# Two expert layers: the low-rank inputs turned between the main tiles, and the last tile in two quarters

## The reference, cut to what matters

```python
x = x + L0_attn(L0_cond(x))
x = x + L0_ffn(L0_cond2(x))      # expert layer 0
x = x + L1_attn(L1_cond(x))
x = x + L1_ffn(L1_cond2(x))      # expert layer 1, the last step

# expert layer 0: 1024 tokens of 512, 8 experts of rank 16, the best 2
gates = relu(layernorm(xf @ gw1.T + gb1) * gamma + beta) @ gw2.T + gb2
top_v, top_i = top_k(gates, 2)
top_g = softmax(top_v)
counts = onehot(top_i).sum(axis=0)        # tokens by expert, over all tokens
w = onehot, weighted by top_g, where counts <= capacity
out = xf @ weight.T + ((xf @ lora_A) * w) @ lora_B * ALPHA

# expert layer 1
combine = the two largest of softmax(x @ W_router.T), divided by their sum
out = x @ W_base.T + b_base + ((x @ A) * combine) @ B * SCALING
```

## Time and profile before

| | |
|---|---|
| median of 3 runs | 1014.01 us (1013.42 to 1014.83) |
| the profiled execution | 1012.35 us, its span 1010.6 us |
| PE busy | 957.1 us (95% of the span) |
| DVE busy | 556.2 us (55%) |
| POOL busy | 469.1 us (46%) |
| ACT busy | 232.3 us (23%) |
| expert layer 0, first main tile to the end of the sixth low-rank product | 652.9 to 686.7 us |
| expert layer 1, first main tile to the first of the final turns | 964.2 to 1003.1 us |

### The profile page before, as it was taken

How to read it: one execution, slowest core, us unless ns; L and a number is a source line. 1 busy time by engine, 2 the same in 40 slices (tenths; PEclk the granted TensorE clock), 3 DMA queues, 4 the chain that set the end, 5 groups by cost and what they waited for, 6 DMA issues and landing times.

```text
span 1010.6 us, 15965 instructions
## 1 busy us (share of the span) xinstructions
PE 957.1 (95%) x6766; PEld 712.3 (70%) x6766; DVE 556.2 (55%) x951; ACT 232.3 (23%) x451; POOL 469.1 (46%) x425
## 2 busy tenths in 40 slices
PE   6899999999999999999999879989989999899997
PEld 2337887877887788887888658846857777446953
DVE  7866748567284753848458435243347969302423
ACT  4602122211122212022120210110052666500001
POOL 7934538485575846758376332301322645220300
PEclk9999999999999999999999989989999999999999
DMA  5782101111110111110113075393470000072002
GB/s 137 177 248 67 57 1 43 73 42 53 43 42 32 42 53 42 73 42 2 53 42 111 17 150 152 84 225 55 185 271 1 3 3 3 2 162 67 4 1 83
DMA packets 36287, 74.30 MB, mean 74 GB/s; under 512 B 13492, under 2 KB 22260, under 8 KB 33140
## 3 DMA queue, kind: packets, MB, share of 16 engines
q1 hardware_dynamic: 35880, 72.89, 25.9%
q10 hardware_dynamic: 336, 0.39, 0.1%
HBM read 66.26 MB, written 7.01 MB: 73 GB/s over the span
## 4 chain that ended last, share of the span: by engine, by line
PE 73%; DVE 11%; POOL 6%; ACT 4%; issue 3%; DMA 1%; SPq 0%; POOLq 0%; DVEq 0%; ACTq 0%
PE ps L1208 15%; PE ps L1146 14%; PE ps L1007 8%; PE ps L1462 5%; PE ps L1280 5%; PE ps L1160 4%; POOL w_lo L2354 3%; DVE arena L2010 3%; ACT acts L1507 2%; PE ps L1385 2%; DVE arena L2007 2%; PE ps L1285 1%; DVE h_lo L2019 1%; PE ps L1387 1%; PE ps L1386 1%
## 5 line engine op out<-in xcount | busy, mean ns | idle before, releaser
L2469 POOL TENSOR_TENSOR arena<-arena 128x512 f32<-128x512 f32 x80 | 103.6, 1295 | 122.7 <-DVE arena L2010 122.6
L1146 PE MATMUL ps<-xt_hi,w_hi 128*128 128x512 f32 x320 | 127.8, 399 | 5.5 <-POOL w_lo L2354 2.7
L1146 PE MATMUL ps<-xt_lo,w_hi 128*128 128x512 f32 x320 | 125.5, 392 | 0.0
L1146 PE MATMUL ps<-xt_hi,w_lo 128*128 128x512 f32 x320 | 125.2, 391 | 0.0
L1208 PE MATMUL ps<-h_hi,wo_hi 128*128 128x512 f32 x256 | 104.9, 410 | 11.9 <-DVE h_lo L2019 11.9
L2028 DVE TENSOR_TENSOR fresh<-ps,fresh 128x512 f32<-128x512 f32 x56 | 38.7, 691 | 133.9 <-PE ps L1208 133.8
L2010 DVE TENSOR_TENSOR arena<-ps,rope 64x512 f32<-64x512 f32 x160 | 110.2, 689 | 2.2
L1208 PE MATMUL ps<-h_lo,wo_hi 128*128 128x512 f32 x256 | 103.1, 403 | 0.0
L1208 PE MATMUL ps<-h_hi,wo_lo 128*128 128x512 f32 x256 | 102.4, 400 | 0.0
L2377 POOL TENSOR_TENSOR xt<-arena 128x512 f32<-128x512 f32 x24 | 30.5, 1270 | 136.9 <-DVE arena L1915 136.9
L1600 ACT ACTIVATE h_hi<-ps 128x512 fp32r<-128x512 f32 x64 | 33.1, 603 | 203.1 <-PE ps L1193 203.1
(11 more groups left out here) (325 smaller groups left out, 1882.8 us busy)
## 6 DMA issues: line engine op xcount, KB each, us to landing
acts<-in_w_o_dram SPq DMA_DIRECT2D x8, 1024.0 KB, 5.0
arena<-in_a_wo_dram SPq DMA_DIRECT2D x8, 1024.0 KB, 5.9
arena<-kernel_rows SPq DMA_DIRECT2D x11, 512.0 KB, 11.7
acts<-in_w_qkv_dram SPq DMA_DIRECT2D x3, 1792.0 KB, 7.0
acts<-in_w_qkv_dram SPq DMA_DIRECT2D x4, 1280.0 KB, 6.6
w_l<-kernel_rows SPq DMA_DIRECT2D x10, 512.0 KB, 11.8
arena<-level_rows SPq DMA_DIRECT2D x4, 1024.0 KB, 21.8
stream<-in_x_dram SPq DMA_DIRECT2D x4, 512.0 KB, 6.7
```

What stands on the lines that cost most here:

```text
L1146: last = pe.matmul(ps[:, bank, :], w[:, r, cols], x, start=(r == 0 and n == 0), stop=(r == R - 1 and n == 2))
L2469: pool.tensor_tensor(qk[:, chunk, half * HALF:(half + 1) * HALF], rot[:, k % 2, 0, :], rot[:, k % 2, 1, :], ALU.add).then_inc(s_rope, 1)
```

## The change

In both expert layers the products keep their number and their operands but for the last tile of layer 1. What changes is where they stand:

- **Layer 0.** `main(0)` to `main(3)`, the count, `main(4)`, the turns of the weighted inputs, `main(5)`, then `lora(0)` to `lora(5)`. The rest is as before.
- **Layer 1.** `main(0)` to `main(2)`, the turns of the weighted inputs, `main(3)`, `lora(0)` to `lora(3)`. Then `main(4)`, turns back of groups 0 and 1, `lora(4)`, `main(5)`, turns back of groups 2 and 3, `lora(5)`. For tile 6 `lora` opens the bank and `main` closes it.
- **Tile 7 of layer 1** is made in two quarters of 256 tokens, low-rank product first: the first in tile 7's bank, the second in tile 4's, behind a wait for tile 4's copy. DVE copies the first (8 samples), ACT the second, with a new instruction. The turn of group 6 waits for that copy.
- On DVE in layer 1 the adds of groups 0 to 3 stand ahead of tile 5's copy, not tile 7's.
- **Output.** Five transfers: three of two groups, then two of one group each.

```diff
--- before.py
+++ after.py
@@ -896,11 +896,12 @@
             load_kernel(3, 2)
             load_levels(3)
             patch(3)
-            for i in range(NGROUP // 2):
-                pair = slice(2 * i * G, 2 * (i + 1) * G)
-                sp.wait_ge(s_added[3], 2 * i + 2)
-                sp.dma_start(out[:, pair, :], stream[:, pair, 1:T + 1]).then_inc(s_out, 16)
-            sp.wait_ge(s_out, 16 * (NGROUP // 2))
+            pieces = (0, 2, 4, 6, 7, 8)
+            for first, end in zip(pieces, pieces[1:]):
+                samples = slice(first * G, end * G)
+                sp.wait_ge(s_added[3], end)
+                sp.dma_start(out[:, samples, :], stream[:, samples, 1:T + 1]).then_inc(s_out, 16)
+            sp.wait_ge(s_out, 16 * (len(pieces) - 1))
 
         N_SETUP = 16 * 3
 
@@ -1274,40 +1275,79 @@
                 for m in range(NTILE):
                     token_products(m)
 
-                def main(k):
+                def main(k, behind=False):
                     half, r_out = k // 4, k % 4
+                    if k in (4, 5):
+
+                        pe.wait_ge(s_natc[n], k - 3)
                     for r in range(R):
-                        pe.matmul(ps[:, FFN_BANK[k], :], w_main[:, r, r_out, :],
-                                  xt[:, r, half * HALF:(half + 1) * HALF], start=(r == 0), stop=False)
-
-                def lora(k):
+                        last = pe.matmul(ps[:, FFN_BANK[k], :], w_main[:, r, r_out, :],
+                                         xt[:, r, half * HALF:(half + 1) * HALF], start=(r == 0 and not behind),
+                                         stop=(r == R - 1 and behind))
+                    if behind:
+                        last.then_inc(s_ffn[n], 1)
+
+                def lora(k, ahead=False):
                     half, r_out = k // 4, k % 4
-                    pe.matmul(ps[:, FFN_BANK[k], :], w_out[:, r_out, :], lora_t[:, half * HALF:(half + 1) * HALF],
-                              start=False, stop=True).then_inc(s_ffn[n], 1)
-
-                for k in range(6):
-                    if k >= 4:
-
-                        pe.wait_ge(s_natc[n], k - 3)
-                    main(k)
-                pe.wait_ge(s_natc[n], 4)
+                    last = pe.matmul(ps[:, FFN_BANK[k], :], w_out[:, r_out, :],
+                                     lora_t[:, half * HALF:(half + 1) * HALF], start=ahead, stop=not ahead)
+                    if not ahead:
+                        last.then_inc(s_ffn[n], 1)
+
+                def last_quarter(q):
+
+                    bank, r_out = (FFN_BANK[7], FFN_BANK[4])[q], R - 1
+                    cols = slice(HALF + q * HALF // 2, HALF + (q + 1) * HALF // 2)
+                    if q:
+                        pe.wait_ge(s_fact[n], 3)
+                    pe.matmul(ps[:, bank, 0:HALF // 2], w_out[:, r_out, :], lora_t[:, cols], start=True, stop=False)
+                    for r in range(R):
+                        last = pe.matmul(ps[:, bank, 0:HALF // 2], w_main[:, r, r_out, :], xt[:, r, cols],
+                                         start=False, stop=(r == R - 1))
+                    last.then_inc(s_ffn[n], 1)
+
+                def turn_weighted():
+                    pe.wait_ge(s_natc[n], 4)
+                    pe.wait_ge(s_lora[n], 1)
+                    for m in range(NTILE):
+                        last = pe.transpose(ps[:, 2 + m // 4, (m % 4) * P:(m % 4 + 1) * P],
+                                            nat[:, m, lora_at:lora_at + P], ident[:, :])
+                        if m % 4 == 3:
+                            last.then_inc(s_lturn[n], 1)
+
                 if n == 0:
+                    for k in range(4):
+                        main(k)
+                    pe.wait_ge(s_natc[n], 4)
                     pe.wait_ge(s_both, 1)
                     pe.matmul(ps[:, 2, 0:P], ones[:, :], both.rearrange("p m k e -> p (m k e)"),
                               start=True, stop=True).then_inc(s_count, 1)
-                pe.wait_ge(s_lora[n], 1)
-                for m in range(NTILE):
-                    last = pe.transpose(ps[:, 2 + m // 4, (m % 4) * P:(m % 4 + 1) * P],
-                                        nat[:, m, lora_at:lora_at + P], ident[:, :])
-                    if m % 4 == 3:
-                        last.then_inc(s_lturn[n], 1)
+                    main(4)
+                    turn_weighted()
+                    main(5)
+                    pe.wait_ge(s_lcopy[n], 2)
+                    for k in range(6):
+                        lora(k)
+                    for k in range(6, 8):
+                        main(k)
+                        turn_first(net, ((s_fact[n], 2), (s_fdve[n], 2)), (2 * k - 12, 2 * k - 11))
+                        lora(k)
+                    return
+                for k in range(3):
+                    main(k)
+                turn_weighted()
+                main(3)
                 pe.wait_ge(s_lcopy[n], 2)
-                for k in range(6):
+                for k in range(4):
                     lora(k)
-                for k in range(6, 8):
+                for k in (4, 5):
                     main(k)
-                    turn_first(net, ((s_fact[n], 2), (s_fdve[n], 2)), (2 * k - 12, 2 * k - 11))
+                    turn_first(net, ((s_fact[n], 2), (s_fdve[n], 2)), (2 * k - 8, 2 * k - 7))
                     lora(k)
+                lora(6, True)
+                main(6, True)
+                for q in range(2):
+                    last_quarter(q)
 
             def attention1():
                 def project(m):
@@ -1484,6 +1524,8 @@
             for what in (s_fact[1], s_fdve[1]):
                 pe.wait_ge(what, 4)
             for g in range(NGROUP // 2, NGROUP):
+                if g == NGROUP - 2:
+                    pe.wait_ge(s_fact[1], 5)
                 turn(3, g)
 
 
@@ -1639,6 +1681,11 @@
                                    ps[:, FFN_BANK[k], :].rearrange("p (b c) -> p b c", c=C),
                                    ACT.Identity, bias=f1_bias[:, 0, r_out:r_out + 1] if n else 0.0)\
                         .then_inc(s_fact[n], 1)
+                if n:
+                    act.wait_ge(s_ffn[n], 9)
+                    act.activation(fresh[:, 24:32, R - 1, :],
+                                   ps[:, FFN_BANK[4], 0:HALF // 2].rearrange("p (b c) -> p b c", c=C),
+                                   ACT.Identity, bias=f1_bias[:, 0, R - 1:R]).then_inc(s_fact[n], 1)
 
             def attention1():
                 def copy_projection(q):
@@ -2189,11 +2236,12 @@
                 (gate0, gate1)[n]()
                 for k in range(1, 8, 2):
                     half, r_out = k // 4, k % 4
-                    for g in range(4 if k == 7 else 0):
+                    for g in range(4 if k == (7, 5)[n] else 0):
                         add_back(2 * n + 1, g)
                     dve.wait_ge(s_ffn[n], k + 1)
-                    dst = fresh[:, half * 16:half * 16 + 16, r_out, :]
-                    src = ps[:, FFN_BANK[k], :].rearrange("p (b c) -> p b c", c=C)
+                    samples = 8 if n and k == 7 else 16
+                    dst = fresh[:, half * 16:half * 16 + samples, r_out, :]
+                    src = ps[:, FFN_BANK[k], 0:samples * C].rearrange("p (b c) -> p b c", c=C)
                     if n:
                         last = dve.tensor_scalar(dst, src, f1_bias[:, 0, r_out:r_out + 1], None, ALU.add)
                     else:
```

## The result

| | before | changed |
|---|---|---|
| median of the runs | 1014.42 us (1013.42 to 1015.97, 4 runs) | 1005.12 us (1001.70 to 1005.42, 4 runs) |
| profiled execution | 1012.35 us, span 1010.6 | 1005.09 us, span 1003.3 |
| layer 0, first main tile to the end of the sixth low-rank product | 33.76 | 27.04 |
| layer 1, first main tile to the first final turn | 38.85 | 36.98 |
| from there to the end of the span | 7.51 | 7.25 |

The ratio is 0.990, with a 95% interval of 0.9884 to 0.9916: the change gains 9.3 us at the median, where 8.8 was forecast. The kernel before has one more run here than the three that the forecast went by; against their 1014.01 the gain is 8.9.

A forecast was written before the change was run, and what follows sets the result against it. The prediction took the tensor engine's chain, 73% of the span, as the bound. Gains of 6.90 (layer 0), 1.90 (layer 1) and 0 (output), 8.80 in all, off the 1014.01 median gave 1005.2 us, range 1003.2 to 1008.3.

The forecast's parts named there:

- Layer 0, 6.90: Expert layer 0, first main tile to last low-rank product: 26.86 us for 33.76, from 3.20 weights standstill, 0.68 copies, 3.03 clock.
- Its third term, 3.03 for the clock: Layer 0's turns (1.98 to 0.87 us) and 12 low-rank passes (7.07 to 5.15) would run at full clock.
- Layer 1, 1.90: Expert layer 1, first main tile to first final turn: 36.95 us for 38.85, a gain of 1.90.
- Behind it, 0: After the first final turn, splitting the output into five transfers gives 0; bounds 0.9 gain, about 0.1 loss.
- What follows moves along: Work behind layer 0, including attention 1's loads, moves 6.9 us earlier; the load queue is free 9.8 us before wanted.
- Rival 5: Attention 1's weights come from a queue still full, layer 0's gain is waited away, 1.9 stays: 1012.1 us, chance 0.02.
- Rival 1: One more fall of the clock elsewhere, as in attention 1, costing about 3.0 us: 1008.2 us, chance 0.15.
- one of the prediction's own signs of being wrong: Signs: layer 0's turns wait beyond some tenths, 256-column passes over 0.22 us, new clock falls, a gap before the last transfer.
- Rival 2: The clock fall at 855 us in attention 1 goes away, worth 1.5 us: 1003.7 us, chance 0.08.
- Rival 3: The half-size last output transfer sets the end, gaining two thirds of 0.9 us: 1004.6 us, chance 0.08.
- Rival 4: Layer 0 gives its standstills but not the clock's 3.0 us: 1008.2 us, chance 0.05.
- Rival 6: Slower: several clock falls at attention 1's heads, 840 to 870 us, at 3.03 each: 1017.3 us, chance 0.02.

The follow-up runs named there:

- e2: Changed kernel with expert layer 0 back in its old order, so only layer 1 and the output change: median 1011.44 us, ratio 0.9975 to the kernel before.
- e3: Kernel before with three unused 512-column products put behind the count of layer 0 to fill the wait: median 1013.08 us, ratio 1.0.
- e10: e3 with four more unused products of 128 columns behind the three, filling the wait longer: median 1013.74 us, ratio 0.9986 to the kernel before.
- e11: The same kernel as e3, run again for another profiled execution: 1009.11 us in that execution, layer 0 31.30 us.
- e1: Kernel before with the new order in expert layer 0 alone: median 1008.13 us, ratio 0.9944 to the kernel before.
- e4: Changed kernel with the output in four transfers of two groups: median 1005.84 us, ratio 0.9915 to the kernel before.
- e9: Changed kernel with two of main tile 4's four products in layer 0 moved behind the turns: median 1006.07 us, ratio 0.9925 to the kernel before.
- e5: Changed kernel with layer 1's tile 7 whole (512 columns), copied by the vector engine alone: median 1005.06 us, ratio 0.9912 to the kernel before.
- e12: The changed kernel again, unaltered, for another profiled execution: span 1002.0 us; the changed kernel's median with it is 1005.09 us.
- e6: Changed kernel with the output in six transfers, groups 4 and 5 sent apart too: median 1003.88 us, ratio 0.9902 to the kernel before.

## Why the prediction was right, point by point

- **Layer 0, 6.90.** Measured 6.72. The order of the pieces came as worked out, and the vector engine's chain ended where it should, with the 0.17 by which the layer began later. What the sum lacked is that the turns' first weight load came only 0.03 ahead of the tile's end, and that cost 0.19. No standstill came of it.
- **Its third term, 3.03 for the clock,** is right in kind in every trace (e2 pays it, e3, e10 and e11 don't), but not all of it is the clock: in e3, at full clock behind the same waits, the turns took 1.09 and the passes 5.42, so the clock's part is 2.5 and 0.5 is the restart behind a wait. The changed kernel won back the restart of the passes (5.15) and not that of the turns (1.06), 2.84 in all. Carried over to medians the term is not confirmed: filling the wait moved the median by 0.4 us at most. The means of all executions, 1013.8 before and 1004.2 changed, are 9.6 apart. By the line above about 6.0 of this is at equal time at half clock, near the standstills of 3.9 and the 2.1 of layer 1 and the end, and 3.6 is for 9.7 us less at half clock (29.8 to 20.1). Of those 9.7, the fall in layer 0 was about 7 in the trace of before (0.93 over 650 to 700, and 1.00 now). But e1, e3 and e10, which are without that fall too in their traces, come down only to 26 us or so. The changed kernel and its variants e4 to e9 have 20.8 over 30 executions, so the low figure is not an accident of five; what brings the rest of it is open. That the forecast for the median came out within 0.1 us is therefore luck in part: the two layers' sums are shown, the account of the clock over the whole execution is not.
- **Layer 1, 1.90.** Measured 1.87. The 256-column passes took 0.216 for 0.215. The last copy's cover held with 0.8 to spare.
- **Behind it, 0.** Measured 0.26. Of this 0.2 is the first add, which starts 0.48 after the first final turn for 0.67, since that turn no longer follows idle time (in e5, where it does, it is 0.67 again). That was missing in the sum. The split of the output was 0, as taken (e4).
- **What follows moves along.** It did: 267.22 before and in e12. Rival 5 is out.
- **Rival 1** happened in the profiled execution, and with it one of the prediction's own signs of being wrong, a fall of the clock where there was none before, for half of its price: 1.4 us for a second fall of about 3.5 us at half clock, not 3.0. The price had been taken from layer 0, where the clock stayed down twice as long. In attention 1, 8 of the 13 kept traces have more than the one fall that the trace of the kernel before has, so a chance of 0.15 for one more was no fit description: such falls move single times by some us, and the median only where their mean number changes. Rival 2 did not happen: no kept trace is without a fall there.
- **Rival 3** falls with e4: four transfers end as late as five. Rival 4's 1008.2 is not what the median came to, but whether all timed executions of the kernel before had the fall in layer 0 is open. Rival 6 was nowhere near.

## What to carry to other kernels

When a helper engine's result is wanted by the tensor engine, don't put all the independent work ahead of the request: ask for the result as soon as its inputs are there, and leave one piece of work for each hand-over. Read a tail of transfers as a block: where it is unbroken, as here, look for what would start it earlier (e6) before cutting the last transfer (e4, nothing). Where single executions of one kernel differ by more than the effect, compare stretches of traces, and note how long the clock was down in each.

## What the runs showed of the hardware

- Every execution spent some of its time at half clock, 14 to 37 us of about 1005. In layer 0 it was full with the engine idle for 1.71 us (e9) and fell with 3.2 (before) and 3.3 (e2).
- The traces of e3, e10 and e11 are without the fall of about 7 us at half clock in layer 0, but their kernels' executions were on average only 3 to 4 us less at half clock. Whether the others have more falls elsewhere or still have that one is open.
- By the line through all executions, a us at half clock costs 0.37 us of time, less than the 0.5 of a tensor engine that never waits. In the traces it was 2.5 us for about 7 in layer 0 and 1.4 for about 3.5 in attention 1.
- A copy of 256 columns from PSUM took 0.48 for 0.75 with 512 on DVE, and 0.47 for 0.69 on ACT: half the columns are two thirds of the time.
